# Attention stage of a two-layer kernel: output gating, second GpSimd operation and first mask rows moved

## The reference

```python
q = (h @ Wq); k = (h @ Wk); v = (h @ Wv)              # per head: q, k of 64, v of 128
# router: each token has a weight rw[r] for 6 experts: two shared, two chosen of four, two zero
qe = einsum(q, Wq_exp) * mask ; ke = einsum(k, Wk_exp) * mask   # mask = (rw != 0)
attn = softmax(qe @ ke.T / 8)                         # for each expert r
o = sum_r rw[r] * (attn @ v)
out = (o * silu(h @ Wg)) @ Wo
```

## Time and profile before

| | |
|---|---|
| timed runs | 2882.95, 2883.83, 2885.61 us; median 2883.83 |
| profiled execution | 2876.81 us, of which the span of its instructions 2875.1 |
| PE / PE weight loads / DVE / ACT / POOL busy in the span | 85% / 58% / 62% / 44% / 39% |
| attention stage | from 361.7 us (first clearing) to about 1110 us |
| looped units of it | 445.40 to about 1010 us |

### The profile page before, as it was taken

The page is one execution under the profiler, slowest core; times in us unless marked ns, Lnnn a source line. Parts: engine busy times, 40 slices in busy tenths (PEclk is TensorE's granted clock), DMA queues, the critical chain, the costliest instruction groups (busy, mean ns, idle before and its releaser), DMA issues. The chain is left out here.

```text
span 2875.1 us, 34327 instructions
## 1 busy us (share of the span) xinstructions
PE 2440.1 (85%) x10156; PEld 1654.3 (58%) x10156; DVE 1780.1 (62%) x2555; ACT 1276.5 (44%) x2546; POOL 1120.5 (39%) x1100
## 2 busy tenths in 40 slices
PE   7999949999999995972999997469898866699989
PEld 5778824444444443851888885335444315588767
DVE  4320239999999995651555553769989986311143
ACT  3222038888888883321555553643232113211121
POOL 0102036666666663535000001348998983111010
PEclk9999969999999997975999998689999998899979
DMA  5263343433433424836777773734444536200032
GB/s 183 78 180 119 95 105 108 111 102 104 122 105 104 123 66 132 311 140 241 229 229 230 228 233 125 233 113 164 171 156 155 178 120 183 66 22 22 8 102 66
DMA packets 269652, 399.91 MB, mean 139 GB/s; under 512 B 33392, under 2 KB 116352, under 8 KB 269536
## 3 DMA queue, kind: packets, MB, share of 16 engines
q1 hardware_dynamic: 234848, 347.64, 38.5%
q10 hardware_dynamic: 28704, 33.08, 3.4%
q0 software_dynamic: 5984, 17.73, 1.8%
HBM read 304.09 MB, written 94.31 MB: 139 GB/s over the span
## 5 line engine op out<-in xcount | busy, mean ns | idle before, releaser
L1021 ACT ACTIVATE attn_probs<-attn_ps_score,attn_nmax 128x512 f32<-128x512 f32 x512 | 343.2, 674 | 17.4 <-DVE attn_nmax L1095 17.4
L2479 PE MATMUL scan_ps_o<-scan_qs,scan_sel 128*128 128x512 f32 x512 | 266.8, 638 | 82.4 <-DVE scan_qs L2423 79.5
L2441 DVE TENSOR_TENSOR_SCAN scan_st<-scan_ps_dec,scan_kv 128x512 f32<-128x512 f32 x256 | 306.0, 1210 | 9.9 <-POOL scan_kv L2393 9.8
L929 PE MATMUL attn_ps_score<-attn_KK,attn_X 64*128 64x512 f32 x512 | 211.9, 465 | 20.3 <-ACT attn_probs L1021 19.8
L1109 DVE SCALAR_TENSOR_TENSOR attn_mixed<-attn_probs,attn_cf,attn_mixed 128x512 f32<-128x512 f32 x256 | 219.7, 858 | 9.1
L2479 PEld LDWEIGHTS scan_ps_o<-scan_qs,scan_sel 128*128 128x128 f32 x512 | 89.0, 194 | 231.4 <-DVE scan_qs L2423 151.3
L1084 DVE TENSOR_REDUCE attn_raw<-attn_ps_score 128x2 f32<-128x1024 f32 x128 | 156.3, 1221 | 55.1 <-PE attn_ps_score L929 54.5
L929 PE MATMUL attn_ps_score<-attn_KL,attn_X 64*128 64x512 f32 x512 | 171.6, 424 | 0.0
L85 POOL MEMSET head_ident<- 128x128 f32 x1 | 0.2, 204 | 439.5 <-POOLq L2827 439.5
L2393 POOL TENSOR_TENSOR scan_kv<-scan_vb,gla_gk 128x512 f32<-128x512 f32 x128 | 160.8, 1280 | 12.4 <-DMA scan_vb<-gv 5.5
L2393 POOL TENSOR_TENSOR scan_kv<-scan_vb,scan_gk 128x512 f32<-128x512 f32 x128 | 159.4, 1287 | 2.4 <-DVE scan_st L2441 2.4
(11 more groups left out here) (438 smaller groups left out, 6833.0 us busy)
## 6 DMA issues: line engine op xcount, KB each, us to landing
scan_vb<-gv SPq DMA_DIRECT2D x256, 256.0 KB
moe_raw<-in_L_ffn_gating SPq DMA_DIRECT2D x92, 512.0 KB
attn_spread<-rows SPq DMA_DIRECT2D x64, 384.0 KB
moe_raw<-in_L_ffn_linear SPq DMA_DIRECT2D x46, 512.0 KB, 5.4
rows_x<-out_zeros SPq DMA_DIRECT2D x23, 512.0 KB, 8.5
moe_xb<-rows_x SPq DMA_DIRECT2D x23, 512.0 KB, 6.2
rows_y<-moe_y ACTq DMA_DIRECT2D x23, 512.0 KB, 6.3
sg<-proj_tile SPq DMA_DIRECT2D x32, 256.0 KB, 2.0
```

The lines of the kernel that those rows point to most:

```text
L929: last = nc.tensor.matmul(ps_score[n][:, j, :], weights, y[p][half, :], start=(r == 0), stop=(r == len(terms) - 1))
L1021: nc.scalar.activation(probs[b][:, at_j, :], ps_score[n][:, j, :], ACT.Exp, bias=nmax[b][:, at_j:at_j + 1], accum_out=Z[b][:, at_j:at_j + ...
L2441: V.tensor_tensor_scan(st[r][:, :], ps_dec[n % 2][:, :], kv[r][:, :], 0.0, ALU.mult, ALU.add).then_inc(st_ready, 1)
L2479: nc.tensor.matmul(ps_o[w][:, :], sel[:, P - GPH - GPH * d:2 * P - GPH - GPH * d], qs[i % RING][:, :], start=(d == 0), stop=(d == HALF - 1 ...
```

## The change

`gate` moves from beside the first maxima of tile 1 to beside those of tile 2, behind the `masked_sums` of tile 1. `beside_maxima` waits for `raw_ready` of the tile and no longer for the first count of `nmax_ready`. The tiles `sel` and `veil` are cleared first, without a wait between the clearings, and `identity` (which the constants end with) counts from the fourth on. SP issues the mask rows of unit 0 behind the inputs and keys of unit 0, as soon as the first two clearings are done, and ahead of the inputs of unit 1.

```diff
-def identity(nc, eng, ident, sem):
+def identity(nc, eng, ident, sem, start=0):
     eng.memset(ident[:, :], 0.0).then_inc(sem, 1)
-    eng.wait_ge(sem, 1)
+    eng.wait_ge(sem, start + 1)
...
-        N_CONST = 6
+        N_SEL0, N_CONST = 2, 6
...
-            for p in two:
-                inputs(p, p, True)
-                keys(p, p, True)
+            inputs(0, 0, True)
+            keys(0, 0, True)
+            sp.wait_ge(const_ready, N_SEL0)
+            mask_rows(0, 0, True)
+            inputs(1, 1, True)
+            keys(1, 1, True)
             sp.wait_ge(const_ready, N_CONST)
-            mask_rows(0, 0, True)
             inputs(0, 2, False)
...
-            identity(nc, nc.gpsimd, ident, const_ready)
-            ch = Chain(pool, const_ready, 2)
-            ch.settle()
+            for x in (sel[0], veil[0], sel[1], veil[1]):
+                nc.gpsimd.memset(x[:, :].bitcast(F32), 0.0).then_inc(const_ready, 1)
+            identity(nc, nc.gpsimd, ident, const_ready, N_CONST - 2)
             for p in two:
-                for x in (sel[p], veil[p]):
-                    ch.link(nc.gpsimd.memset(x[:, :].bitcast(F32), 0.0))
                 nc.gpsimd.memset(o[p][:, :], 0.0).then_inc(o_free[p], 16)
-                pool.wait_ge(o_free[p], 16)
...
             def beside_maxima(u, t):
-                pool.wait_ge(nmax_ready, (u * TT + t) * 2 + 1)
+                pool.wait_ge(raw_ready, u * TT + t + 1)
...
                 masked_sums(u, 0)
-                if not first:
-                    beside_first_maxima(u, 1, False)
-                    gate(i - 1, p, u - 2)
                 if left(u) >= 1:
                     beside_maxima(u, 1)
                     low_keys(i + p, 1 - p, u + 1)
                 masked_sums(u, 1)
+                if not first:
+                    beside_first_maxima(u, 2, False)
+                    gate(i - 1, p, u - 2)
```

## The result

The kernel after takes 2908.64 us (median of 4 runs, 2905.19 to 2915.65) against 2883.39 of before (2882.69 to 2885.61): a ratio of 1.0089, interval 1.0067 to 1.0111. It is slower, by 25.3 us; forecast were 2906 and +22. The spans therefore differ by 34.7 us, more than the medians.

A forecast was written before the change was run, and what follows sets the result against it. VectorE, busy 545.8 of 564.6 us in the loop, was taken as the bound. Profiled 2876.8 + 25 (loop) - 7.3 (start) + 4 (clock) = 2898.5, plus 7.0 to the timed median: 2905.5, forecast 2906 us, range 2893 to 2922.

The forecast's parts named there:

- step 2: Third tile step of a looped unit, with the moved gating: a tie VectorE wins, 0; +1.15 us if GpSimd is first.
- the clock: PE's granted clock in the loop: more waiting, so dips to 1.2 GHz cost +4 us; bounds -4 and +10.
- step 0: First tile step of a looped unit: GpSimd's second operation holds VectorE's coefficients, +1.05 us a unit.
- step 1: Second tile step of a looped unit: gating's move gains 1.15 us, low keys hold coefficients 1.06; net -0.09.
- rest of step 3: Fourth tile step of a looped unit: its second GpSimd operation waits for ScalarE's copy, not `min`; 0.
- unrolled units 28 to 31 and the end: Among six unrolled units outside the loop: each step could go either way, taken at 0; bounds for all six -7, +9 us.
- start, to unit 2: Start of the attention stage: earlier mask rows start tile 1 at 400.4 instead of 407.72, -7.3 us; bounds -10, -3.
- the rival with all three steps held: Looped units: GpSimd also wins the tie in step 2, 30 us more plus some clock dips: 2938 us; chance 0.24.
- the clock rival: Loop: a PE clock dip in every unit instead of eight in all, 22 us more: 2928, up to 2950; chance 0.08.
- No stall: Attention units: VectorE's small operations pass before GpSimd; step 1 gains 34.5 us over 30 units: 2842 us; chance 0.18.

The follow-up runs named there:

- release_only: The kernel before with only the second GpSimd operation released by the raw maxima, the gating left in its old place: 2947.18 us, ratio 1.0223.
- the last run: The changed kernel released by `min` again, with the awaited waits of gating, both step-3 subtractions and also the choosing passed last: 2834.92 us, ratio 0.9836.
- the one ahead of it: The changed kernel released by `min` again, with the awaited waits of the gating and both step-3 subtractions passed last, not the choosing's: 2834.39 us, ratio 0.9825.

## Why the prediction was right, and where its sizes were off

The direction, the mechanism and the total came out; two terms did not, step 2 and the clock: step 2 came out 11.8 us above its forecast, the clock 6.5 us below. That the total lies within 3 us is luck to that extent. Terms over the stage of the profiled executions, us:

| term | predicted | measured |
|---|---|---|
| step 0, 26 units | +27.3 | +25.8 |
| step 1 without dips | -2.3 | -3.9 |
| step 2 | 0 | +11.8 |
| clock | +4 | -2.5 |
| rest of step 3 | 0 | +0.6 |
| unrolled units 28 to 31 and the end | 0 | -2.1 |
| start, to unit 2 | -7.3 | -4.9 |
| stage | +21.7 | +24.7 |

(The first five, the terms of the loop, are rounded; the loop's span grew by 31.7.)

*Step 0* was worked out to 1.05 and is 0.99: the second operation starts at 469.21, 0.13 before the coefficients, where 0.14 was read off.

*Step 1* was to be a wash, and is. Predicted was a low-keys start 0.10 before the coefficients; it is 0.12. (The 1.06 taken for the hold is a little small by the prediction's own way of working: with the 0.03 us of step 0 behind 474.86, and the second maxima of before at 473.81, it is 1.08, 0.5 us over the loop.) The gain from the gating's move, put at 1.15, is 1.16 when it stands alone.

*Step 2* is the mis-sized term. It was called a tie and taken as 0; measured is +0.45 a unit: 13 odd units are 1.01 longer and 13 even ones 0.10 shorter than before. The bound of +1.15 covered it. What failed is the start taken for GpSimd's first operation in this step and, with it, the race. The gating was to start 0.32 to 0.40 after the raw maxima in every unit and to end behind the waiting `min`. That is so in the even units (0.32), and there VectorE did pass first; with the choosing's other waits out of the way it no longer did, which bears out the reason given, that GpSimd still has waits to pass. In the odd units the gating starts at 0.07 and ends as `min` is due (1.37), and the choosing is there at 1.40, before the coefficients. Nor does the gating decide: an earlier one changes nothing, and release_only has the same starts without any. What decides is how long the choosing takes to pass its other waits after `raw_ready`: 1.40 or 1.59 us after the raw maxima's start. The trace of before has the same difference, +1.69 and +1.88 in this step, but behind `min`, where it did not hold the small operations; the prediction's working for this step treats all units alike. So the rival with all three steps held was half true.

*The clock* was given the wrong sign. The reason, PE will wait more, holds, and there are six dips instead of four. But each costs 0.31 us of wait instead of 0.93, because it falls into a step that is a microsecond longer than VectorE's work anyway. The kernel with the choosing's wait last has both kinds in one loop: waits of about 0.31 behind a held step 1, and of 0.90 to 1.10 behind a free step 3. (In the clock rival 22 more dips were counted; from eight to one in each of the 26 looped units they are 18.)

*The start* moved tile 1 by 7.6 us, predicted 7.3. Two sizes in it were off and nearly cancelled: the four issues ahead delayed the choosing for unit 1 by 0.5 us and not 1.5 (31.8 into the stage instead of 31.2), and from PE's expansion to the raw maximum it took 5.2 us and not 4.75. 2.7 of the gain went back in units 0 and 1: the first has steps of 12.40, 6.03, 6.42 and 5.80, the second a coefficient operation held in steps 0 and 2. The unrolled units, taken at 0, are held in part: units 28 and 29 in step 2 only, which the 1.07 gained in step 1 pays for, unit 30 nowhere.

*No stall* (2842) describes the version with the old release well: 2838.15. The prediction rightly tied it to VectorE passing before GpSimd.

Why the two halves of the loop body differ by 0.18 us is narrowed down and not settled. The difference goes when the choosing passes its three other waits before the awaited one (1.62 and 1.64 in the last run, 1.89 and 1.73 in the one ahead of it), so it lies in the time for those waits. Which of them takes longer in one half, and why, no run shows.

## What to carry to other kernels

When a GpSimd operation is released beside VectorE's work, look not at what ends when it may start but at what VectorE issues next: if a small operation with two SBUF inputs follows, release GpSimd after it, since 0.22 us gained on an engine with time to spare (a start 1.40 instead of 1.62 after the raw maxima's, in step 0) cost 1.0 us on the bound one, and the release cost 70 us here (2908.6 against 2838.2) with nothing in return. In the groups of a profile, a tiny operation whose maximum equals the length of another engine's operation is the sign. Read more than one unit before you call a race a tie: here every second one went the other way. And measure the parts of a bundled change apart: a gain of 39 us and one of 7 were hidden under this one.

## What the runs showed of the hardware

- A VectorE operation of 0.16 us with two SBUF inputs took 1.15 to 1.30 us behind a GpSimd tensor operation of 1.27 to 1.30 and ended with it; 0.64 behind one of half the columns; 0.16 beside a clearing of 0.53 that only writes.
- VectorE's pair `min` and coefficients is not protected as a pair: GpSimd gets in between them (469.21 between 469.19 and 469.34) and so holds the second one alone.
- Where `min` was already waiting for a gating that ended 0.26 us later, it got in at that end, and GpSimd's next operation followed at once (0.27 and 0.28 us in two kernels). Where `min` came 0.01 us before the gating's end and the choosing was recorded 0.04 us before `min`, the choosing got in and `min` took 1.25. Recorded starts 0.01 to 0.02 us apart don't tell who was first.
- GpSimd came 0.18 to 0.19 us later to the same operation in one half of the loop body than in the other, unit after unit, in the kernels before and after and in the one with the release alone (before: 1.88 and 1.69), and within 0.02 us of it in both (1.62 and 1.64) where its other waits came first. In the kernel after that decided 12 us.
- A stretch of PE at the lower clock cost VectorE 0.93 us of waiting where its step was tight, 0.31 at the end of a step that was held anyway, and up to 2.32 in the tight step 3 of the version with the release alone.
